# Key gathers of a graph-attention kernel: static batches of twelve tiles that land in the score buffer, two batches ahead

## What is computed

```python
def rgat_conv(x, W, q, k, b, src, dst, etype, heads, out_ch, n_nodes):
    xr = jnp.einsum('nd,rdf->rnf', x, W)
    oi = xr[etype, dst]
    oj = xr[etype, src]
    qi = oi @ q
    kj = oj @ k
    alpha = jax.nn.leaky_relu(qi + kj, NEG_SLOPE)
    m = jax.ops.segment_max(alpha, dst, num_segments=n_nodes)
    e = jnp.exp(alpha - m[dst])
    z = jax.ops.segment_sum(e, dst, num_segments=n_nodes)
    a = e / (z[dst] + EPS)
    msg = (a[:, :, None] * oj.reshape(-1, heads, out_ch)).reshape(-1, heads * out_ch)
    out = jax.ops.segment_sum(msg, dst, num_segments=n_nodes)
    return out + b
...
h = jnp.maximum(_layernorm(x, axis=-1), 0.0)
x = x + _L0_gnn_ref(h, edge_index, L0_gnn_W, L0_gnn_b)
h = jnp.maximum(_layernorm(x, axis=-1), 0.0)
x = x + _L1_gnn_ref(h, edge_index, edge_type_3, ...)
```

## Time and profile before

| | us |
|---|---|
| median of three runs | 1900.07 |
| the three runs | 1898.57, 1900.07, 1923.51 |
| span of the profiled execution, from its first to its last instruction | 1928.8 |
| busy in it: PE / DVE / POOL / ACT | 1612.4 / 969.4 / 1108.7 / 171.8 |
| key gathers (L424): number, busy | 348, 381.1 |
| row gathers (L405): number, busy | 504, 493.1 |

### The profile page before, as it was taken

One profiled execution on the slowest core, in us unless ns is written; L12 is line 12 of the kernel. 1 busy time (PEld: TensorE's weight loads), 2 busy tenths in 40 slices (PEclk: granted clock), 3 DMA queues, 4 the chain that ended last, 5 costly groups with the idle time before them and its releaser, 6 DMA issues.

```text
span 1928.8 us, 31024 instructions
## 1 busy us (share of the span) xinstructions
PE 1612.4 (84%) x7380; PEld 1073.4 (56%) x7384; DVE 969.4 (50%) x2495; ACT 171.8 (9%) x345; POOL 1108.7 (57%) x1454
## 2 busy tenths in 40 slices
PE   2797978889887995689868887887898899799996
PEld 2664634444486553355557777785555555444443
DVE  6798643444420667778855555551433444222232
ACT  0110111111110110000000011111011011000000
POOL 0793556666501677777746665441477777466664
PEclk9987989999955998778879999885799799899999
DMA  5222058777730122111157776554012011588787
GB/s 208 101 97 78 37 177 246 245 236 241 241 110 3 42 70 64 26 26 35 35 160 238 241 219 183 178 173 103 26 50 99 25 46 46 171 256 261 248 261 264
DMA packets 86255, 268.24 MB, mean 139 GB/s; under 512 B 31483, under 2 KB 31858, under 8 KB 86198
## 3 DMA queue, kind: packets, MB, share of 16 engines
q0 software_dynamic: 51456, 199.20, 34.7%
q1 hardware_dynamic: 34742, 68.27, 10.1%
HBM read 235.88 MB, written 31.52 MB: 139 GB/s over the span
## 4 chain that ended last, share of the span: by engine, by line
PE 44%; POOL 21%; issue 18%; DVE 8%; DMA 4%; DVEq 1%; another core or an unknown queue 1%; POOLq 1%; ACT 1%; SPq 1%; ACTq 0%; PEldq 0%
POOL kb L424 17%; PE ps L1094 10%; PE ps L1008 9%; PE ps L1096 6%; PE ps L1097 6%; PE ps L955 3%; DMA ring<-rows,idxs 2%; PE ps L985 2%; PE ps L982 2%; DVE stage L632 2%; PE ps L1018 2%; DMA wreg<-in_L_gnn_W 2%; DVE zw L868 1%; PE ps L1027 1%
## 5 line engine op out<-in xcount | busy, mean ns | idle before, releaser
L405 POOL DMA_INDIRECT ring<-rows,idxs x504 | 493.1, 978 | 337.1 <-issue 138.4
L1055 PE MATMUL ps<-wreg,hT 128*128 128x384 f32 x1440 | 496.7, 508 | 7.5 <-PEq L1048 6.6
L424 POOL DMA_INDIRECT kb<-keys,kidx x348 | 381.1, 1095 | 134.9 <-issue 88.4
L1055 PEld LDWEIGHTS ps<-wreg,hT 128*128 128x128 f32 x1440 | 285.5, 200 | 207.7 <-issue 33.1
L1094 PE MATMUL ps<-ring,zw 128*128 x1328 | 249.4, 346 | 52.6 <-DVE zw L868 41.8
L1008 PE MATMUL ps<-ring,zw 128*128 x664 | 238.8, 503 | 40.1 <-DVE zw L699 31.0
L1094 PEld LDWEIGHTS ps<-ring,zw 128*128 128x128 f32 x1328 | 230.1, 200 | 73.0 <-issue 69.6
L795 DVE TENSOR_TENSOR hn<-hn,al 128x1024 f32 (+1 forms) x166 | 137.2, 827 | 234.3 <-POOL al L437 155.4
L1008 PEld LDWEIGHTS ps<-ring,zw 128*128 128x128 f32 x664 | 114.7, 192 | 119.5 <-issue 75.0
L1096 PE MATMUL ps<-ring,zw 128*128 x332 | 141.8, 509 | 27.8 <-DVE zw L870 17.4
L868 DVE TENSOR_TENSOR zw<-zw,al 128x512 f32<-128x512 f32 x166 | 113.7, 692 | 92.7 <-PE ps L1094 83.5
(11 more groups left out here) (165 smaller groups left out, 1466.5 us busy)
## 6 DMA issues: line engine op xcount, KB each, us to landing
wreg<-in_L_gnn_W SPq DMA_DIRECT2D x12, 2304.0 KB, 10.3
rows<-stage SPq DMA_DIRECT2D x30, 386.0 KB
rows<-stage SPq DMA_DIRECT2D x30, 384.5 KB
ring<-rows,idxs POOLq DMA_INDIRECT x504
kb<-keys,kidx POOLq DMA_INDIRECT x348
rows<-wreg SPq DMA_DIRECT2D x10, 384.0 KB, 3.1
xs<-in_x SPq DMA_DIRECT2D x3, 1152.0 KB, 10.1
out_x<-xs SPq DMA_DIRECT2D x9, 384.0 KB
```

What stands on the lines that cost most here:

```text
L405: nc.gpsimd.indirect_dma_start(ring[:, s, 0:WIDTH[l]], None, rows[l], bass.IndirectOffsetOnAxis(idxs[:, s:s + 1], 0)).then_inc(g_sem[l][s] ...
L424: nc.gpsimd.indirect_dma_start(kb[:, side, s, 0:H], None, keys[l], bass.IndirectOffsetOnAxis(kidx[:, side, s:s + 1], 0)).then_inc(k_in[l][ ...
L1055: last = mm(ps[:, 2 * (nt % 2) + h, 0:HALF], hT[:, k, nt * P:(nt + 1) * P], wreg[:, r % 2, k, h * HALF:(h + 1) * HALF], start=(k == 0), st ...
```

## The change

Keys are no longer gathered into a tile of their own: an indirect DMA lands in the slots of `al`, reads its indices straight from `idxr`, and the score is computed in place with one helper tile `low`. Batches hold twelve edge tiles instead of six, and the loop over batches is written out: KBATCHES = 15 of them for all 180 edge tiles, whatever `bnd` says. Two batches are asked for before POOL waits for `qs_ready`, and each later one two batches ahead, with three semaphores in turn. DVE's wait after the maxima is for all NPAIR pairs.

```diff
-KB = 2 * PAIRS_STEP
+KB = 4 * PAIRS_STEP
+KBATCHES = 2 * NPAIR // KB
+KSEMS = 3
+assert KBATCHES * KB == 2 * NPAIR
...
-        kidx = sb("kidx", [P, 2, 2 * PAIRS_STEP], I32)
...
-        kb = sb("kb", [P, 2, 2 * PAIRS_STEP, 4])
...
-        atmp = sb("atmp", [P, 2, KB * 4])
-        btmp = sb("btmp", [P, 2, KB * 4])
-        ctmp = sb("ctmp", [P, 2, KB * 4])
+        low = sb("low", [P, KB * 4])
...
-                def ask_keys(side, batch, n):
-
-                    nc.gpsimd.tensor_copy(kidx[:, side, :], idxr[:, ds(batch * KB, KB)]).then_inc(k_ix, 1)
-                    pool.wait_ge(k_ix, n)
-                    pool.sem_inc(turn, 1)
-                    for s in range(KB):
-                        nc.gpsimd.indirect_dma_start(kb[:, side, s, 0:H], None, keys[l], bass.IndirectOffsetOnAxis(kidx[:, side, s:s + 1], 0)).then_inc(k_in[l][side], 16)
-
-                def score(side, g):
-
-                    batch = 2 * g + side
-                    pool.wait_ge(k_in[l][side], 16 * KB * g + 16 * KB)
...
+                def ask_keys(n):
+
+                    for t in range(n * KB, (n + 1) * KB):
+                        nc.gpsimd.indirect_dma_start(al[:, t * H:(t + 1) * H], None, keys[l], bass.IndirectOffsetOnAxis(idxr[:, t:t + 1], 0)).then_inc(k_in[l][n % KSEMS], 16)
+
+                def score(n):
+
+                    batch = al[:, n * KB * H:(n + 1) * KB * H]
+                    pool.wait_ge(k_in[l][n % KSEMS], 16 * KB * (n // KSEMS + 1))
+                    nc.gpsimd.tensor_tensor(batch, batch, qs[:, n * KB * H:(n + 1) * KB * H], ALU.add).then_inc(k_sum[l], 1)
+                    pool.wait_ge(k_sum[l], n + 1)
+                    nc.gpsimd.tensor_scalar(low[:, 0:KB * H], batch, 0.0, SLOPE, ALU.min, ALU.mult).then_inc(k_low[l], 1)
+                    nc.gpsimd.tensor_scalar(batch, batch, 0.0, None, ALU.max).then_inc(k_low[l], 1)
+                    pool.wait_ge(k_low[l], 2 * n + 2)
+                    nc.gpsimd.tensor_tensor(batch, batch, low[:, 0:KB * H], ALU.add).then_inc(al_step[l], KB // 2)
 
                 pool.wait_ge(s_keys, 16 * R * l)
-                ask_keys(0, 0, kix_count + 1)
+                ask_keys(0)
+                ask_keys(1)
                 pool.wait_ge(qs_ready, l)
-                with pool.Fori(0, batches2) as g:
-                    ask_keys(1, 2 * g + 1, kix_count + (2 * g + 2))
-                    score(0, g)
-                    ask_keys(0, 2 * g + 2, kix_count + (2 * g + 3))
-                    score(1, g)
-                pool.wait_ge(k_in[l][0], 16 * KB * batches2 + 16 * KB)
-                pool.sem_inc(turn, 1)
-                kix_count = kix_count + (2 * batches2 + 1)
+                for n in range(KBATCHES):
+                    score(n)
+                    if n + 2 < KBATCHES:
+                        ask_keys(n + 2)
...
-                dve.wait_ge(al_step[l], 6 * batches2)
+                dve.wait_ge(al_step[l], NPAIR)
```

More of the change, by code:

```diff
@@ L237, in gnn_kernel @@
         qs_ready = sem("qs_ready")
-        k_in = {l: [sem(f"k_in{l}_{i}") for i in range(2)] for l in (1, 2)}
-        k_used = {l: sem(f"k_used{l}") for l in (1, 2)}
-        k_ix = sem("k_ix")
+        k_in = {l: [sem(f"k_in{l}_{i}") for i in range(KSEMS)] for l in (1, 2)}
+        k_sum = {l: sem(f"k_sum{l}") for l in (1, 2)}
+        k_low = {l: sem(f"k_low{l}") for l in (1, 2)}
         al_step = {l: sem(f"al_step{l}") for l in (1, 2)}
         nm_step = {l: sem(f"nm_step{l}") for l in (1, 2)}
-        b_used = {l: sem(f"b_used{l}") for l in (1, 2)}
         m_chain = {l: sem(f"m_chain{l}") for l in (1, 2)}
@@ L412, in _ @@
             ix_count = 2 * groups
-            kix_count = 0
             for l in (1, 2):
                 H = HEADS[l]
-                batches2 = (bnd[NT] + (2 * PAIRS_STEP - 1)) // (2 * PAIRS_STEP)
-                def ask_keys(side, batch, n):
-                    nc.gpsimd.tensor_copy(kidx[:, side, :], idxr[:, ds(batch * KB, KB)]).then_inc(k_ix, 1)
-                    pool.wait_ge(k_ix, n)
-                    pool.sem_inc(turn, 1)
-                    for s in range(KB):
-                        nc.gpsimd.indirect_dma_start(kb[:, side, s, 0:H], None, keys[l], bass.IndirectOffsetOnAxis(kidx[:, side, s:s + 1], 0)).then_inc(k_in[l][side], 16)
-                def score(side, g):
-                    batch = 2 * g + side
-                    pool.wait_ge(k_in[l][side], 16 * KB * g + 16 * KB)
-                    nc.gpsimd.tensor_tensor(atmp[:, side, 0:KB * H].rearrange("p (c h) -> p c h", h=H), qs[:, ds(batch * (KB * H), KB * H)].rearrange("p (c h) -> p c h", h=H), kb[:, side, :, 0:H], ALU.add).then_inc(k_used[l], 1)
-                    pool.wait_ge(k_used[l], batch + 1)
-                    pool.sem_inc(turn, 1)
[L434 to L437, removed]
```

## The result

The changed kernel took 2011.9 us (median of 4 runs, 2000.4 to 2026.9) against 1911.8 us before (4 runs, 1898.6 to 1927.4): a ratio of 1.054, interval 1.048 to 1.060. The prediction was 1847. All ratios here are of fast runs: an execution over 1.5% above the fastest of its kernel counts as slow and stands outside them.

The account below looks back on a forecast made before the run. POOL's key gathers were taken to lead layer 1, with DVE and PE following, and PE to bound layer 2. Savings of 38 + 16 = 54 us of 1928.8, or 53 from 1900.1, gave 1847; range 1829 to 1879.

Parts of the forecast that it names:

- layer 1's period: Layer 1 scoring: 20.0 us per batch of twelve gathers, 22.3 where a node tile ends; layer 1 saves 38 us.
- POOL's last batch that counts: Layer 1 scoring: its keys are scored and ready at 910.5 us, against 963.1 before.
- rival (4): Gathers miss their gap beside DVE's tensor_tensors, one per two of them: slower, 2058 us; chance 0.06.
- rival (3): Gathers run free of DVE, which becomes the bound; layer 1 saves 53.6 and layer 2 17: 1830 us; chance 0.09.
- layer 2: Layer 2 scoring: POOL's period falls to 17 us and PE's waits for DVE go; saves 16 us, bounds 10 and 18.
- Twenty-four gathers at 1.25 are 30 us from 587 us on: Before layer 1's queries: two batches asked early fit POOL's idle time, ending at 617; head start 8 us.
- All waits of PE for DVE go: Layer 2 scoring: PE's waits of 10.84 and 1.56 us vanish.
- (2): Nothing reaches the end: PE's fixed stops and clock, or written-out code's instruction fetch; 20 us or less, 1885; chance 0.10.

Follow-up runs that it names:

- f2: The kernel before, unaltered, run again on a third chip: 1889.2 us, ratio 1.004.
- f1: The changed kernel, unaltered, run again on a third chip: 1802.9 us, ratio 0.956.
- e4: The kernel before with its loop over key batches written out, still in sixes, nothing else changed: 1932.4 us, ratio 1.004.

## Why the prediction was wrong

*Right: layer 1's period.* 20.0 us was forecast and 20.0 measured, and 19.5 to 21.1 later, where node tiles end and I had taken 22.3. So POOL's last batch that counts is ready 264 us after the queries, 15 sooner than the 279 worked out (910.5 less 631.7). The stretch from the ready queries to L804 takes 306.8 us (657.3 to 964.1) all the same; the forecast was 309.8 (631.7 to 941.5). POOL no longer ends it: PE's last transposes start at 955.2 without a wait, and DVE waits 1.4 us for them. That the sum came out within 3 us is in part luck, since it went by POOL's path, with an error of 15 us there, and PE's was as long. DVE's waits for `al`, 61.4 us in the earlier trace rows, fell to 11.7. The gaps between gathers stayed at 0.30, so rival (4), the slower one, didn't happen (its 2058 stands near the 2011.9 by chance, from another cause); and the gathers beside DVE's tensor_tensors stayed at 1.22 us, so rival (3) didn't either.

*Right in kind, wrong in size: layer 2, where nothing is held up.* I took 16 us, and it was 28.7 (f2 against f1). PE's two waits go, 11.79 and 2.86 us there. The rest, some 14 us, I had put at 2 to 4: this is the term that was too small. About half of it stands in three rows of projecting matmuls that are 1.5, 3.0 and 2.7 us shorter; the rest lies in the spreads between them, which come in fewer pieces. The timeline of f2 with the stop

```profile
1463.19 0.66 PE L1073 MATMUL ps<-ident,zw 128*128 128x128 f32 x2 [11.79 <-DVE mx L770]
1463.64 24.88 PE L1055 MATMUL ps<-wreg,hT 128*128 128x384 f32 x72
...
1535.68 18.73 PE L1055 MATMUL ps<-wreg,hT 128*128 128x384 f32 x48
```

and that of f1 without it:

```profile
1395.51 0.38 PE L1059 MATMUL ps<-ident,zw 128*128 128x128 f32 x2
1395.73 23.39 PE L1041 MATMUL ps<-wreg,hT 128*128 128x384 f32 x72
...
1463.57 15.74 PE L1041 MATMUL ps<-wreg,hT 128*128 128x384 f32 x48
```

The windows of the two rows of 48 show the clock as the difference, f2 at 0.84

```profile
1536.00:1554.00 18.00, 18.00 (x48) 10.24 (x48) 8.09 (x30) 1.47 (x3) 12.71 (x22) 0.84 0.07 23
```

and f1 at the full 1.00:

```profile
1464.00:1479.00 15.00, 15.00 (x48) 8.87 (x47) 5.85 (x20) 1.47 (x3) 11.51 (x15) 1.00 0.13 43
```

That the wait of 11.79 us is what slowed this row isn't shown: f2's row of 48 in between, from 1516.78 us on, took 15.72 us, as in f1, and what stands just before the slow one is a spread in two pieces.

In all 43.4 + 28.7 + 2.2 us of the stretches and spreads are won on that chip, 74 for my 54; the two stages that the change doesn't touch give back 5.4, which leaves 69 from the first spreads to the end (1325.7 us to 1256.8). The spans differ by 83, of which 14.0 were there before the first key gather; on the five chips without hold-up the unaltered first stage lasts from 543 to 573 us, so that part isn't the change's. Even there the measured 1802.9 lies under the 1829 at which my range ends.

*Wrong, and decisive: "Twenty-four gathers at 1.25 are 30 us from 587 us on, so they end at 617, before 631.7."* The sum took the 631.7 as fixed, and gathers beside PE's spreads as free. It is the same assumption as "All waits of PE for DVE go" in layer 2: that POOL's gathers can't reach PE but by `al`. Where the prediction was tested they do, by way of issue, at 24.3 + 17.1 + 105.9 us; the 16 us of layer 2 that the sum counts as won became a loss of 105.9. None of my rivals had it: (2) comes nearest, with a stall that costs as much as is saved, but lays it to the written-out code, and e4 rules that out. Yet it stood in the trace of before, in the spreads beside layer 1's six early gathers, a place that the sum passes over, since PE waits for nobody there:

```profile
590.63 0.98 PE L985 MATMUL ps<-q,stT 128*128 128x12 bf16 x16 [0.38 <-issue]
591.97 0.23 PE L985 MATMUL ps<-q,stT 128*128 128x12 bf16 x3 [0.36 <-issue]
...
594.85 0.24 PE L985 MATMUL ps<-q,stT 128*128 128x12 bf16 x3 [1.15 <-issue]
...
597.02 2.00 PE L985 MATMUL ps<-q,stT 128*128 128x12 bf16 x36 [0.34 <-issue]
```

(Between 821 and 827 us it has single issues once more.) Six early gathers cost PE 3.5 us there (45.6 for 42.1). Four times as many would have given 14 us in that stage by proportion, and dense gathers in layer 2 a rival slower than before. f2 on a chip without hold-up has no such rows.

## What to carry to other kernels

Before gathers are moved beside another engine's work, look in the trace of before at that engine's rows wherever gathers already run: matmuls issued singly with "issue" in front of them are a price that grows with the length of the row. Where it shows, keep rows short: six gathers and 2.2 us of other work between them cost layer 2 nothing, twelve with 2.3 us cost 58. Pauses inside a long row were never tried where the issue is held up. And where a result contradicts a mechanism that its own trace confirms, run the unaltered kernel again elsewhere before experimenting further; here the sign of the change depends on it.

## What was not expected of the hardware

- On some chips (or at some times) a row of small indirect gathers by GpSimd holds up instruction issue on TensorE and VectorE: single instructions start at multiples of 0.70 us, register instructions take 0.70 us, with DMA engines 4% busy. Six, twelve and twenty-four gathers in a row cost 3.5, 11.5 and 28 us in the same 42 us of work. On five other chips twenty-four cost nothing (41.5 to 42.1 us). What holds the issue up is open.
- Rows of twelve in which a gather starts every 1.5 us (layer 1) didn't hold up the projecting matmuls beside them (a stretch of 311.1 us for 309.5); rows of twelve at 1.25 us (layer 2) did.
- Those executions also move 6 to 10% less in large row gathers (235 to 243 against 259 to 261 GB/s).
- A starved PE pays twice: the granted clock was 0.53 in the held-up stretch, and a projecting matmul took 799 ns for 491.
